# The output stage of an attention block written out step by step, with the next stage's loads and zeros inside it

## What is computed

```python
x = x + _layernorm(_L0_attn_ref(_layernorm(x, axis=-1), ...), axis=-1)   # attention, ends in  out @ Wo + bo
x = x + _layernorm(_L0_ffn_ref(_layernorm(x, axis=-1), ...), axis=-1)    # six layers of local attention + gated FFN
```

```python
y  = o @ Wo + bo
x2 = x + (y - mean(y)) / sqrt(var(y) + 1e-05)      # kept for the end of the kernel too
x3 = (x2 - mean(x2)) / sqrt(var(x2) + 1e-05)       # the input of the six layers
```

## Time and profile before

| | |
|---|---|
| median of 3 runs | 4478.52 us (4476.37 to 4480.85) |
| the profiled execution | 4480.28 us, of which span 4478.4 us |
| mean granted TensorE clock | 0.968 of full |
| output stage, first to last instruction | 957.2 to 1029.4 us |
| `layers`, first data instruction | 1042.9 us |
| busy share of the span | PE 93%, PEld 66%, DVE 83%, ACT 80%, POOL 52% |

### The profile page before, as it was taken

One profiled execution on the slowest core, in us unless ns is written; L12 is line 12 of the kernel. 1 busy time (PEld: TensorE's weight loads), 2 busy tenths in 40 slices (PEclk: granted clock), 3 DMA queues, 4 the chain that ended last, 5 costly groups with the idle time before them and its releaser, 6 DMA issues. The chain is left out here.

```text
span 4478.4 us, 137304 instructions
## 1 busy us (share of the span) xinstructions
PE 4185.3 (93%) x44000; PEld 2964.7 (66%) x44000; DVE 3697.2 (83%) x8420; ACT 3591.3 (80%) x6842; POOL 2342.0 (52%) x2840
## 2 busy tenths in 40 slices
PE   4899999966999999999999999999999999999994
PEld 2466666643777777777777777777777777777773
DVE  6688888876888888888888888888888888888884
ACT  1799998944888888888888888888888888888882
POOL 1000000016766666666766666666666666666661
PEclk7899999977999999999999999999999999999996
DMA  6777777722111111111111111111111111111111
GB/s 224 219 234 230 228 226 229 234 77 70 37 45 41 44 37 38 45 41 45 35 40 44 41 45 35 43 41 41 45 35 43 40 41 45 36 42 40 45 40 49
DMA packets 258776, 359.63 MB, mean 80 GB/s; under 512 B 44404, under 2 KB 216156, under 8 KB 257884
## 3 DMA queue, kind: packets, MB, share of 16 engines
q1 hardware_dynamic: 258140, 351.55, 26.0%
HBM read 151.19 MB, written 93.34 MB: 55 GB/s over the span
## 5 line engine op out<-in xcount | busy, mean ns | idle before, releaser
L1369 PE MATMUL la_ps<-la_Wqkv,la_xsT 128*128 (+1 forms) x2304 | 1195.1, 614 | 6.4 <-DVE la_rsk L1083 3.5
L1026 POOL TENSOR_TENSOR la_rt<-la_rt,la_rn 128x1024 f32<-128x1024 f32 x384 | 722.9, 1904 | 27.5
L1083 DVE TENSOR_TENSOR la_rsq<-la_ps,la_tab 128x1024 f32<-128x1024 f32 x384 | 469.3, 1222 | 104.5 <-ACT la_sq L1227 101.4
L1227 ACT ACTIVATE la_sq<-la_ps 128x512 f32<-128x512 f32 x768 | 454.5, 596 | 90.1 <-PE la_ps L1369 28.2
L1090 DVE TENSOR_REDUCE la_ssum<-la_sq 128x8 f32<-128x512 f32 x768 | 502.3, 673 | 24.0 <-issue 24.0
L1404 PEld LDWEIGHTS la_ps<-la_kT,la_qB 128*64 128x64 f32 x12288 | 391.3, 138 | 146.1 <-issue 145.8
L1369 PEld LDWEIGHTS la_ps<-la_Wqkv,la_xsT 128*128 128x128 f32 x2304 | 378.1, 191 | 150.4 <-issue 109.7
L1083 DVE TENSOR_TENSOR la_rsk<-la_ps,la_tab 128x1024 f32<-128x1024 f32 x384 | 465.1, 1211 | 4.7 <-ACT la_sq L1227 4.4
L1435 PEld LDWEIGHTS la_ps<-la_Wo,la_oT 128*128 128x128 f32 x3072 | 366.7, 192 | 131.1 <-issue 130.3
L1404 PE MATMUL la_ps<-la_kT,la_qB 128*64 128x64 f32 x12288 | 434.1, 224 | 0.0
L475 POOL COPY at_vh<-V 128x64 f32 (+1 forms) x64 | 15.2, 238 | 785.6 <-PE at_ps L674 784.8
(11 more groups left out here) (168 smaller groups left out, 10272.7 us busy)
## 6 DMA issues: line engine op xcount, KB each, us to landing
at_band<-skew_scratch SPq DMA_DIRECT2D x64, 1536.0 KB, 7.3
la_vs<-la_v SPq DMA_DIRECT2D x192, 384.0 KB, 3.5
skew_scratch<-at_R SPq DMA_DIRECT2D x64, 1024.0 KB, 6.7
la_vs<-la_v SPq DMA_DIRECT2D x192, 128.0 KB, 3.4
la_Wqkv<-in_wqkv SPq DMA_DIRECT2D x28, 384.0 KB, 3.3
kt_scratch<-pr_k SPq DMA_DIRECT2D x24, 384.0 KB, 3.2
qt_scratch<-pr_q SPq DMA_DIRECT2D x24, 384.0 KB, 4.1
at_qh<-qt_scratch SPq DMA_DIRECT2D x64, 144.0 KB
```

The source lines that it names most:

```text
L1026: e.tensor_tensor(heads(rt, w), heads(rt, w), wide(rn[:, w * H:(w + 1) * H], D), ALU.mult)\
L1083: e.tensor_tensor(dst.rearrange("p f (h d) -> p f h d", d=D), ps[:, c % 2, :].rearrange("p (h d) -> p h d", d=D).unsqueeze(1).to_broadcast ...
L1227: e.activation(sq[:, c % 2, :], ps[:, c % 2, :], ACT.Square).then_inc(sq_ev.sem, 1)
L1369: e.matmul(ps[:, c % 2, :], xsT[:, m * P:(m + 1) * P], Wqkv[:, ds(layer(n) % 2, 1), c * 512:(c + 1) * 512], start=True, stop=True)\
```

## The change

The output stage moves inside `layers`: the Part of `layers` is opened first, and `first_output` runs in a block of its own within it, so that the large tiles of `layers` exist while it runs. X2 now lives to the end; `rsq` and `rsk` of `layers` are laid over it, and the output stage uses `vs` of `layers` as its `oT` and `yn`.

- No loops: the 8 steps are written out, and `oT`, `yn`, the norms' statistics and the PSUM banks have two buffers each.
- POOL's copy to `oc` is gone (PE transposes X2 itself).
- The bias is a product on PE: a row of ones times `bo4`, 128 x 512, with the four products by Wo accumulated on it. DVE's add of the bias is gone, and the statistics read PSUM.
- Both norms' application moves to ACT as `Identity` with scale and bias from SBUF, eight 128 x 128 instructions a step; DVE makes -mean*rstd for them (`shifted`).
- The sum X + yn moves to POOL.
- SP issues the 20 loads of `layers` behind Wo and bo4; POOL does its zeroing a piece a step (`zeros`), DVE casts the constants at the stage's end (`casts`), and ACT loads the function table at its start.

```diff
-            def body(t):
-                for i, m in t.back(0):
-                    e.wait_ge(t_mm.sem, t_mm.v(i - 1))
-                    e.tensor_copy(oc[:], X2[:, ds(i * G, G), :]).then_inc(oc_ev.sem, 1)
...
+        oT, yn = (room[:, u, :].rearrange("p (u c) -> p u c", u=2) for u in range(2))
+                loads(e)
+                for i in range(STEPS):
+                    e.wait_ge(x2_ev.sem, x2_ev.v(i))
+                    e.dma_start(x2_d[:, i * G:(i + 1) * G, :], X2[:, i * G:(i + 1) * G, :]).then_inc(s_x2, 16)
...
+                zeros(e, 0)
+                for i in range(STEPS + 2):
+                    for n, u in steps(i, 0):
+                        ln1[u].root(e, n // 2)
+                    for n, u in steps(i, 1):
+                        e.wait_ge(yn_ev.sem, yn_ev.v(n))
+                        x = X[:, slot(n * G):slot(n * G) + G, :].rearrange("p g d -> p (g d)")
+                        e.tensor_tensor(x2(n), x, yn[:, u, :], ALU.add).then_inc(x2_ev.sem, 1)
+                    for n, u in steps(i, 2):
+                        ln2[u].root(e, n // 2)
+                    for n, u in steps(i, 0):
+                        zeros(e, n + 1)
...
+                        e.matmul(ps[:, BANK_Y + u, :], one[:], bo4[:], start=True, stop=False)
+                        for g in range(G):
+                            mm = e.matmul(ps[:, BANK_Y + u, cols(g)], oT[:, u, cols(g)], Wo[:], start=False, stop=g == G - 1)
...
+                    for n, u in steps(i, 1):
+                        e.wait_ge(mr_ev[0].sem, mr_ev[0].v(n))
+                        if n >= 2:
+                            e.wait_ge(x2_ev.sem, x2_ev.v(n - 2))
+                        for g in range(G):
+                            act = e.activation(yn[:, u, cols(g)], ps[:, BANK_Y + u, cols(g)], ACT.Identity,
+                                               bias=mr[:, 0, u, g, :], scale=ln1[u].st[:, g, 8:9])
...
+                for i in range(STEPS + 3):
+                    for n, u in steps(i, 0):
+                        ...
+                        ln1[u].take(e, [ps[:, BANK_Y + u, cols(g)] for g in range(G)], n // 2)
+                    for n, u in steps(i, 3):
+                        shifted(ln2[u], 1, n, u)
+                    for n, u in steps(i, 2):
+                        ...
+                        ln2[u].take(e, [X2[:, n * G + g, :] for g in range(G)], n // 2)
+                    for n, u in steps(i, 0):
+                        shifted(ln1[u], 0, n, u)
+                casts(e)
...
+        def zeros(e, i):
+            if i == 0:
+                e.memset(Y[:].rearrange("p a b -> p (a b)"), 0.0)
...
-            e.memset(kT[:].rearrange("p a b -> p (a b)"), 0.0)
-            e.memset(Y[:].rearrange("p a b -> p (a b)"), 0.0)
-            e.memset(v[:].rearrange("p a b -> p (a b)"), 0.0)
```

More of the change, by code:

```diff
@@ L178, in build @@
         ident = top.enter_context(nc.sbuf_tensor("ident", [P, P], F32))
[L179 to L184, removed]
+        X2 = top.enter_context(nc.sbuf_tensor("X2", [P, NT, E], F32))
+        with nc.sbuf_tensor("V", [P, NT, E], F32) as V:
+            first_projections(nc, a, X, V, ident, qt_d, kt_d, rel_d, skew)
+            first_attention(nc, a, V, X2, ident, qt_d, kt_d, rel_d, skew)
+        layers(nc, a, X, X2, ident, x2_d)
         last_output(nc, X, x2_d, out)
@@ L737, in _, with first_output @@
             rounds(e, body, HEADS_A, RING_A, DEEPEST_A)
[L740 removed]
+def first_output(nc, a, X, X2, ident, x2_d, ps, room, loads, zeros, casts):
     STEPS = NT // G
     with Part(nc, "ou") as t:
[L744 to L770, removed]
[L772 to L842 removed]
@@ L845, in layers @@
-def layers(nc, a, X, ident):
+        Wo, bo4, one = t.sb("Wo", [P, E]), t.sb("bo4", [1, G * E]), t.sb("one", [1, P])
+        oT, yn = (room[:, u, :].rearrange("p (u c) -> p u c", u=2) for u in range(2))
+        mr = t.sb("mr", [P, 2, 2, G, 1])
+        s_in, s_one, s_x2 = t.sem("in"), t.sem("one"), t.sem("x2")
+        t_mm, oT_ev, o_mm = t.mark("tm"), t.mark("oT"), t.mark("om")
+        yn_ev, x2_ev, x_ev, mr_ev = t.mark("yn"), t.mark("x2e"), t.mark("xe"), [t.mark(f"mr{w}") for w in range(2)]
@@ L847, in layers @@
+def layers(nc, a, X, X2, ident, x2_d):
     with Part(nc, "la") as t:
@@ L856, in layers @@
         tab = t.sb("tab", [P, RING_T, 2, 2, D])
-        rsq, rsk, rt = t.sb("rsq", [P, 2, INNER]), t.sb("rsk", [P, 2, INNER]), t.sb("rt", [P, 2 * INNER])
+        rsq, rsk = (X2[:, w * NT // 2:(w + 1) * NT // 2, :].rearrange("p (u a) d -> p u (a d)", u=2) for w in range(2))
+        rt = t.sb("rt", [P, 2 * INNER])
         unit = t.sb("unit", [P, 1])
@@ L913, in two, with loads @@
             return x.rearrange("p (k d) -> p k d", k=2)
-        @block.sync
-        def _(e):
-            for mark in vs_in + ys_in:
-                mark.open(e)
+        def loads(e):
             for dst, src in ((lng, "lngT"), (lnb, "lnbT"), (b1, "b1T"), (mask32, "c_mask"), (rot, "c_rot")):
@@ L938, in next_layer, with casts, _ @@
+        def casts(e):
+            e.memset(xsT[D:P, 0:1], 0.0).then_inc(s_set, 1)
+            e.wait_ge(s_in, 16 * N_IN)
+            e.tensor_copy(mask[:], mask32[:])
+            e.tensor_copy(identb[:], sq[:, 0, 0:P]).then_inc(s_mask, 1)
+        first_output(nc, a, X, X2, ident, x2_d, ps, vs, loads, zeros, casts)
+        block = t.block()
+        @block.sync
+        def _(e):
+            for mark in vs_in + ys_in:
+                mark.open(e)
             def next_layer(n, m):
@@ L941, in next_layer @@
                     e.wait_ge(f_mm.sem, f_mm.v(n // NT * (NT // 2) - 1))
-                    load(n // NT + 1, n // TB % B)
+                    load(e, n // NT + 1, n // TB % B)
             def w1_in(n, m):
```

158 lines of the change are left out of this document (91 added, 67 removed).

## The result

| | before | after |
|---|---|---|
| median | 4478.24 us (4476.37 to 4480.85, 4 runs) | **4515.14 us** (4511.39 to 4519.70, 4 runs) |
| ratio | | **1.0082** (95% interval 1.0065 to 1.0100) |
| span of the profiled execution, clock | 4478.4 us, 0.968 | 4516.9 us, 0.968 |

The account below looks back on a forecast made before the run. DVE was taken to bound the output stage, with POOL the bound after the change. Stage 16.2 plus seam 12.9 make 29.1 us, so the median should be 4449.4 us, range 4441 to 4461.

Parts of the forecast that it names:

- The step that failed: Steady layers: instructions and waits stay, the new place of rsq and rsk costs nothing, with 2 us allowed either way.
- the last of the signs named for the prediction being wrong: Span from the first xc to the end: the prediction is wrong if it isn't the old 3435.5 us.
- The stage: Output stage: POOL becomes the bound, at 5.8 us a step with zeroing; it ends at 1013.1, 16.2 us sooner.
- The named sign: Output stage: DVE's L119 and L844 wait for POOL, with medians well over 0.17 and 0.2 us.
- my sum: Output stage: four DVE instructions take turns with POOL's four, 5.1 + 0.7 = 5.8 us a step; by the skill's rule some 5.6.
- The seam: Between output stage and layers: ACT starts 2.0 us behind the stage's end against 14.9, so 12.9 us sooner.
- the bound of 11.4 that was named: Seam: the gain is 11.4 us if ACT's and PE's semaphore openings take twice DVE's 1.5.
- The sum: Whole kernel: 16.2 from the stage and 12.9 from the seam make 29.1 us, for a median of 4449.4 us.
- The rivals: Whole kernel: no turns or fast PE, 4442 (0.12); gain given back, 4454 to 4466 (0.09); no overlap (0.04); nothing hidden, 4462 (0.05).
- An unseen loss in the layers: Layers: a reason for a slower kernel, without a size; slower had 0.05, shared with the serial rival.
- the serial rival: Output stage: steps don't overlap, each runs its 15.8 us chain nearly alone; the kernel takes 4522 us; chance 0.04.

Follow-up runs that it names:

- e1: The changed kernel with two one-element memsets more on POOL at the end of its part of attention: 4472.64 us, 0.9977 of the kernel before.
- e7: The changed kernel with two memsets more on POOL, rsq and rsk in tiles of their own, and rt, pr and oT over X2: 4470.55 us, 0.9973.
- e9: The changed kernel with two memsets on POOL, 136 instructions more on PE in the output stage, and rt, pr and oT over X2: 4464.78 us, 0.9958.
- e4: The kernel before the change with X2 kept allocated to the end and rsq and rsk laid over it: 4487.46 us, 1.0013.
- e2: The changed kernel with 120 one-element memsets more on POOL at the end of its part of attention: 4468.68 us in a single run.
- e11: The kernel before the change with 9 one-element memsets more on POOL at the end of its part of attention: 4514.84 us, 1.0076.
- e13: The kernel before with 9, 116, 39 and 70 instructions more on POOL, PE, DVE and ACT, and rsq and rsk over X2: 4542.14 us, 1.0136.
- e12: The kernel before with 9, 116, 39 and 70 instructions more on POOL, PE, DVE and ACT at the end of attention: 4537.38 us, 1.0122.
- e14: The kernel before with 116 satisfied waits more on PE alone at the end of attention: 4493.01 us, 1.0024.
- e10: The changed kernel with rt, pr and oT over X2 and 119, 136, 89 and 58 instructions more on POOL, PE, DVE and ACT: 4462.66 us, 0.9956.

## Why the prediction was wrong

**The step that failed** is the last sentence on the seam: "Steady layers keep their instructions and waits; that `rsq` and `rsk` lie elsewhere costs nothing in any row, and I allow 2 us either way for it." The instructions and waits are kept, their time is not: from the first `xc` to the end the kernel took 4516.9 - 1016.7 = 3500.2 us and not the old 3435.5, which was the last of the signs named for the prediction being wrong. What isn't kept is where the instructions lie in the code, which the sum left out. From the changed kernel's side the 64.2 us come apart so: 44.1 are POOL's pause behind its branch (after to e1), 1.9 the other choice of tiles (e1 to e7), 10.4 PE's packets (e7 to e9), and 7.8 are left, of the size of X2's 7.5 (e4). The pause is shown by taking it away (e1, e2) and by making it in the old kernel (e11). That PE's place counts is shown by e9; that it does so through packets that meet Y's copy rests on their times. The 1.9 are too small to be told from nothing.

**What stays open.** Put into the old kernel, the same causes give 48.2 us (e13) of the 64.2. Where the other 16 lie the traces tell, from one write of Y to the next: about 7 behind the 4th tile, where PE's packet meets Y's copy more often in the changed kernel than in e12 to e14, 6 behind the 15th, in which POOL's branch lies and where the root comes 0.5 us later than in e11 to e13, and near 3 behind the 11th. Why is open. One rival wasn't tried: PE's head in e12 to e14 is 3 or 4 instructions short of the changed kernel's, and on POOL one instruction decided between 13.6 and 30.5 us.

**The stage** (forecast 1013.1): 1015.5, of which 1.7 are the later end of attention. POOL is the bound, as forecast. A step is 5.1 to 5.3 us and not 5.8, since POOL hardly pauses between its instructions: what waits is DVE. The named sign was a median well over 0.17 for L119 and over 0.2 for L844. L119 has 0.295, L844 only 0.166; their longest (1.18 and 1.23) end with an instruction of POOL, as forecast. The rule cited from the Trainium skill ("SBUF — State Buffer", "Who interferes with whom") was nearer to this than my sum, and the trace agrees: the three L844 of 1.2 us fall on POOL's addition, the one that meets a zeroing by itself (at 970.1) takes 0.167, and the four of 0.2 to 0.6 in a zeroing stand behind an L119 that ends with it.

**The seam** (forecast 12.9): from the stage's end to the first copy 3.0 us, not 2.0, against 14.9: 11.9 us. PE's eleven semaphore openings take 0.15 us each, so that its transpose starts 2.3 us behind the end and not 1.5; this lies within the bound of 11.4 that was named. No load is waited for, and no packet of code moves there (1013 to 1019.5). Loads, zeros and casts are hidden, as forecast.

**The sum** of the two was 29.1; by the traces it is 25.7, or 27.4 if counted from attention's end. With the layers' share taken back as far as it was (e10), the kernel is 19.5 us faster than the one before on the same chip, within 3 us of the forecast 29.1 less X2's 7.5.

**The rivals.** None of them is what happened. "An unseen loss in the layers" stood among the reasons for slower, with 0.05 for it and the serial rival together, and had no mechanism or price. The trace of before had signs of both the taken branch and the code that is loaded, a row of its waits (1400 to 4200 us) and one of its page:

```profile
PEld la_ps L1358 <- issue: 28.4, 10, 3.2
```

```profile
q14 instruction: 286, 2.34, 0.2%
```

PE waits for issue once in each turn, at its branch, and a queue brings code all the time. I read neither as a thing that the change could move.

## What to carry to other kernels

Code that is added or written out ahead of a long loop moves the loop's head and every edge behind it in the stream of code, on each engine by its own number of instructions. After such a change compare the length of a turn and the first rows behind the taken branch before looking anywhere else, and if an engine waits there for "issue", try two instructions more ahead of the loop: here that was worth 44 us of the layers, more than the whole change had to give. A step that is moved or unrolled for 25 us should be measured with the heads put back, since otherwise its own gain can't be told from this.
